# Next batch's preparation on VectorE placed in other blocks of a sparse-attention and expert layer

## The reference

```python
x = x + attention(layernorm(x)); x = x + experts(layernorm(x))

# attention: 8 blocks of 64 tokens; each query block sees itself and its best key block per head
c = einsum(mean of q per block, mean of k per block) * SCALE         # 8 x 8 per head
block_mask = (c >= top-1 of the row) | eye(8)
probs = softmax(where(block_mask, q @ k.T * SCALE, -inf)); out = (probs @ v) @ proj_w.T + proj_b

# experts: 4 experts with 512 hidden features, the 2 best per token
logits = x @ wr + br; gates = softmax(top 2 of logits)
y_e = gelu(x @ w1_e + b1_e) @ w2_e + b2_e
out = sum over the 2 chosen of gate * (y_e - c_e + c_sum)            # c: constants of the biases
```

## Time and profile before

| | |
|---|---|
| median of 3 runs | 943.72 us (943.45 to 947.8) |
| the profiled execution | 946.72 us, of which the span is 945.0 |
| TensorE, matmuls | 876.3 us busy (93% of the span) |
| TensorE, weight loads | 578.6 us (61%) |
| VectorE | 555.0 us (59%) |
| ScalarE | 459.4 us (49%) |
| GpSimd | 181.9 us (19%) |
| mean granted TensorE clock | 0.977 |
| chain that ended last | TensorE 58%, VectorE 15%, issue 10%, DMA 7%, SyncE's queue 5%, ScalarE 3% |

### The profile page before, as it was taken

The page is one execution under the profiler, slowest core; times in us unless marked ns, Lnnn a source line. Parts: engine busy times, 40 slices in busy tenths (PEclk is TensorE's granted clock), DMA queues, the critical chain, the costliest instruction groups (busy, mean ns, idle before and its releaser), DMA issues.

```text
span 945.0 us, 24244 instructions
## 1 busy us (share of the span) xinstructions
PE 876.3 (93%) x9638; PEld 578.6 (61%) x9638; DVE 555.0 (59%) x1554; ACT 459.4 (49%) x740; POOL 181.9 (19%) x183
## 2 busy tenths in 40 slices
PE   3797899999999999999999999999999999999995
PEld 2475666666657666665656666665756666575662
DVE  7445647475675747566574757567474756736321
ACT  1332463645537363644637364463736455373640
POOL 5601110212121121212111121212112121211111
PEclk8797999999999999999999999999999999999998
DMA  7440442615345260625426062533516153350110
GB/s 208 114 135 20 116 132 58 175 34 152 102 117 142 76 167 23 173 80 139 120 78 181 14 190 60 148 110 90 168 40 184 40 148 97 98 149 2 57 57 14
DMA packets 96022, 99.40 MB, mean 105 GB/s; under 512 B 8969, under 2 KB 82705, under 8 KB 95905
## 3 DMA queue, kind: packets, MB, share of 16 engines
q1 hardware_dynamic: 93168, 85.09, 32.5%
q0 software_dynamic: 2544, 12.58, 4.3%
q10 hardware_dynamic: 192, 0.13, 0.1%
HBM read 48.10 MB, written 28.71 MB: 81 GB/s over the span
## 4 chain that ended last, share of the span: by engine, by line
PE 58%; DVE 15%; issue 10%; DMA 7%; SPq 5%; ACT 3%; POOL 1%; DVEq 0%; POOLq 0%; ACTq 0%
PE y_ps L403 14%; PE s_ps L310 8%; PE o_ps L346 5%; SPq L1120 5%; PE s_ps L259 4%; PE s_ps L261 4%; PE s_ps L260 4%; DVE rmax L661 4%; DMA kv<-kv_chosen 3%; ACT hid L949 2%; PE s_ps L335 2%; DMA selected<-kv_table,index 2%; PE v_ps L319 2%; PE v_ps L326 2%; PE a_ps L376 2%
## 5 line engine op out<-in xcount | busy, mean ns | idle before, releaser
L403 PE MATMUL y_ps<-hid,w2s 128*128 128x512 f32 x480 | 240.8, 602 | 0.0
L913 ACT ACTIVATE prob<-s_ps 128x1024 f32<-128x1024 f32 x128 | 131.1, 1024 | 185.4 <-PE s_ps L335 185.4
L661 DVE TRANSPOSE_TENSOR_REDUCE rmax<-s_ps 128x16 bf16<-128x512 f32 x256 | 168.6, 701 | 58.8 <-PE s_ps L310 58.6
L949 ACT ACTIVATE hid<-s_ps,b1s 128x512 f32<-128x512 f32 x256 | 171.1, 688 | 36.5 <-PE s_ps L261 36.0
L310 PE MATMUL s_ps<-qdiag,kv 64*128 64x512 f32 x768 | 134.7, 456 | 7.2 <-DMA kv<-kv_chosen 4.5
L670 DVE TENSOR_REDUCE nmax<-v_ps 128x64 bf16<-128x256 bf16 x128 | 54.0, 422 | 105.4 <-PE v_ps L326 105.4
L259 PE MATMUL s_ps<-xnhi,w1hi 128*128 128x512 f32 x256 | 112.0, 437 | 1.5
L906 ACT COPY vaug<-v_ps 128x128 f32<-128x128 f32 x128 | 34.0, 265 | 162.1 <-PE v_ps L319 156.2
L1049 POOL TENSOR_TENSOR yT<-yT,gate_cols 128x512 f32<-128x512 f32 x48 | 61.6, 1282 | 259.0 <-DVE gate_cols L757 258.6
L310 PEld LDWEIGHTS s_ps<-qdiag,kv 64*128 64x128 f32 x768 | 85.6, 254 | 34.5 <-ACT hid L949 10.6
L261 PE MATMUL s_ps<-xnhi,w1lo 128*128 128x512 f32 x256 | 101.2, 395 | 0.0
(11 more groups left out here) (149 smaller groups left out, 1117.5 us busy)
## 6 DMA issues: line engine op xcount, KB each, us to landing
gate_cols<-gates SPq DMA_DIRECT2D x64, 256.0 KB, 5.2
kv_table<-stage SPq DMA_DIRECT2D x16, 768.0 KB, 3.9
kv<-stage SPq DMA_DIRECT2D x16, 768.0 KB, 6.4
kv_chosen<-selected SPq DMA_DIRECT2D x15, 768.0 KB, 5.3
kv<-kv_chosen SPq DMA_DIRECT2D x15, 768.0 KB, 4.9
qdiag<-qpair SPq DMA_DIRECT2D x504, 16.0 KB
xs<-in_x SPq DMA_DIRECT2D x16, 256.0 KB, 4.4
out_x<-x SPq DMA_DIRECT2D x16, 256.0 KB, 4.8
```

Of the source, the lines that this page charges most:

```text
L403: ins = pe.matmul(dst[:], w2s[:, n, :], hid[:, n, :], start=(c == 0), stop=(c == C - 1))
L661: v.tensor_reduce(rmax[m % 2][:, :, half * P // 2:half * P // 2 + HH].rearrange("p k h -> p h k"), s_ps[m % 2][:, half * N:(half + 1) * N] ...
L913: act.activation(prob[m % 2][:].rearrange("p h s -> p (h s)"), s_ps[m % 2][:], ACT.Exp, scale=SCALE).then_inc(exped, 1)
L949: act.activation(hid[:, k, :], up_ps[up_bank(k)], ACT.Gelu, bias=b1s[:, k:k + 1]).then_inc(gelued, 1)
```

## The change

On VectorE, for b from 1 to 14: a_stats moves from block 0 of the batch before use to the burst one batch earlier (for batch b+2 in the burst of b, between o_project(b, 2) and o_rows(b, 3); for b = 0 behind c_stats). a_rows moves from block 1 (ahead of block_max) to block 0, behind block_max. q's sum and split go from the head of block 3 to block 2 behind block_max and ahead of o_rows; k's from the head of block 4 to block 3 behind block_max; a_select from the head of block 6 to block 5 behind block_max; `qk` goes from block 5 to block 4 and stays ahead of block_max. c_logits goes from block 2 to block 1 behind block_max; a_columns stays in block 1 but ahead of c_gated. c_gates, c_split and c_gates_turned each go one block later. On TensorE the q, k and v projections go from the end of blocks 2, 3 and 4 to behind shift and o_project, a_columns goes between the two c_down of block 1, and a_products goes from the end of block 5 to the end of block 4. GpSimd's inverse and c_split follow. SyncE issues two placements of q fewer ahead of put_selected, two more between it and take_selected, and sends the gates' five transfers after all placements. ScalarE's code is the same.

```diff
--- before.py
+++ after.py
@@ -239,7 +239,7 @@
         def stages(b):
 
 
-            return (2, 0, 1, 3) if b == 0 else (2, 3, 4, 5)
+            return (2, 0, 1, 3) if b == 0 else (2, 3, 4, 4)
 
         def taken(b):
 
@@ -484,8 +484,12 @@
                         o_columns(b, (m - 3) // 2)
                     if m in (4, 6):
                         o_project(b, (m - 4) // 2)
+                    if b >= 1 and b + 1 < B and m in stages(b)[:3]:
+                        project(b + 1, "qkv"[stages(b).index(m)])
                     if b >= 2 and not edge:
                         c_down(b - 2, 2 * m)
+                    if b >= 1 and b + 1 < B and m == 1:
+                        a_columns(b + 1)
                     if m in (2, 4, 6):
                         o_rows(b, (m - 2) // 2)
                     if b >= 2:
@@ -495,9 +499,7 @@
                     if b >= 1 and m == 0:
                         c_route(b - 1, (0, 1))
                     if b + 1 < B:
-                        if b >= 1 and m == 1:
-                            a_columns(b + 1)
-                        if m in stages(b)[:3]:
+                        if b == 0 and m in stages(b)[:3]:
                             project(b + 1, "qkv"[stages(b).index(m)])
                         if m == stages(b)[3]:
                             a_products(b + 1)
@@ -807,14 +809,11 @@
             a_columns(1)
             block_max(0, 0)
             for b in range(B):
+                ahead = b >= 1 and b + 1 < B
                 for m in range(M):
                     row_max(b, m)
-                    if b + 1 < B:
+                    if b == 0:
                         q_at, k_at, _, products_at = stages(b)
-                        if b >= 1 and m == 0:
-                            a_stats(b + 1)
-                        if b >= 1 and m == 1:
-                            a_rows(b + 1)
                         if m == q_at + 1:
                             q_total = a_q_sum(b + 1)
                             a_q_parts(b + 1)
@@ -824,39 +823,53 @@
                             a_qk(max(q_total, k_total))
                         if m == products_at + 1:
                             tied = a_select(b + 1)
-                    if b == 0 and m == 6:
-                        bias_out()
-                    if b == 0 and m == 7:
-                        bias_sum()
-                    if b >= 1:
-                        if m == 1:
-                            c_route(b - 1)
-                        if m == 2:
-                            ranked = c_logits(b - 1)
+                        if m == 6:
+                            bias_out()
+                        if m == 7:
+                            bias_sum()
+                    if b >= 1 and m == 1:
+                        c_route(b - 1)
+                    if ahead and m == 4:
+                        a_qk(max(q_total, k_total))
                     if m + 1 < M:
                         block_max(b, m + 1)
                     if m in (4, 6):
                         o_project(b, (m - 4) // 2)
+                    if ahead and m == 0:
+                        a_rows(b + 1)
+                    if b >= 1 and m == 1:
+                        ranked = c_logits(b - 1)
+                    if ahead and m == 1:
+                        a_columns(b + 1)
+                    if ahead and m == 2:
+                        q_total = a_q_sum(b + 1)
+                        a_q_parts(b + 1)
+                    if ahead and m == 3:
+                        k_total = a_k(b + 1)
                     if m in (2, 4, 6):
                         o_rows(b, (m - 2) // 2)
+                    if ahead and m == 5:
+                        tied = a_select(b + 1)
+                    if b >= 1 and m == 4:
+                        c_gates(b - 1, ranked)
+                    if b >= 1 and m == 6:
+                        c_split(b - 1)
+                    if b >= 1 and m == 7:
+                        c_gates_turned(b - 1)
                     if b >= 2 and m % 2:
                         c_gated(b - 2, m // 2)
                     if b == 0 and m == 2:
                         bias_masked()
-                    if b >= 1 and b + 1 < B and m == 1:
-                        a_columns(b + 1)
-                    if b >= 1 and m == 3:
-                        c_gates(b - 1, ranked)
-                    if b >= 1 and m == 5:
-                        c_split(b - 1)
-                    if b >= 1 and m == 6:
-                        c_gates_turned(b - 1)
                 o_project(b, T - 2)
-                if b == 0 and b + 1 < B:
+                if b == 0:
                     block_max(b + 1, 0)
+                if b >= 1 and b + 2 < B:
+                    a_stats(b + 2)
                 o_rows(b, T - 1)
                 o_project(b, T - 1)
                 c_stats(b)
+                if b == 0:
+                    a_stats(b + 2)
                 c_rows(b)
                 if b >= 2:
                     c_add(b - 2)
@@ -1064,21 +1077,23 @@
             for b in range(B):
                 for m in range(M):
                     if b + 1 < B:
-                        if b >= 1 and m == 0:
-                            inverse(b + 1, mv, veps, rstd, mean_done, rstd_done)
                         if b >= 1 and m == 1:
                             a_rows(b + 1)
                         if m == stages(b)[3] + 1:
                             a_select(b + 1)
                     if b == 0 and m < E:
                         split_w1(m)
-                    if b >= 1 and m == 5:
-                        c_split(b - 1)
                     if b >= 2 and m in (4, 6):
                         c_sum(b - 2, m // 2 - 1)
+                    if b >= 1 and m == 6:
+                        c_split(b - 1)
                 if b >= 2:
                     c_sum(b - 2, E - 1)
+                if b >= 1 and b + 2 < B:
+                    inverse(b + 2, mv, veps, rstd, mean_done, rstd_done)
                 inverse(b, mv2, veps2, rstd2, mean2_done, rstd2_done)
+                if b == 0:
+                    inverse(b + 2, mv, veps, rstd, mean_done, rstd_done)
             b = B - 1
             c_split(b)
             for e in range(1, E):
@@ -1179,23 +1194,20 @@
                         a_v(b + 1, bank_a, bank_a)
                     place_q(b + 1, 0, range(8, H))
                     if b >= 1:
-                        place_q(b + 1, 1, range(4))
+                        place_q(b + 1, 1, range(2))
                     put_selected(b + 1)
-                if b >= 1:
-                    put_gates(b - 1)
                 if b == 0:
                     take_selected(b + 1)
                     place_q(b + 1, 1, range(9))
                 elif b + 1 < B:
-                    place_q(b + 1, 1, range(4, 9))
+                    place_q(b + 1, 1, range(2, 9))
                     take_selected(b + 1)
-                if b >= 1:
-                    for e in range(E - 1):
-                        take_gate(b - 1, e)
                 if b + 1 < B:
                     place_q(b + 1, 1, range(9, H))
                 if b >= 1:
-                    take_gate(b - 1, E - 1)
+                    put_gates(b - 1)
+                    for e in range(E):
+                        take_gate(b - 1, e)
             b = B - 1
             store(b - 2)
             put_gates(b)
```

## The result

The changed kernel takes 949.41 us (median of 10 runs, 947.7 to 951.29) against 943.72 for the kernel before (10 runs). The ratio is 1.0064, 95% interval 1.0052 to 1.0077: slower by about 6 us. Forecast were 950.0 (936 to 961) and slower.

What follows compares the result with a forecast made beforehand. TensorE was taken as the bound, so only stalls could be won: 13 steady batches x 0.83 = 10.8, less 4.5 for the chosen keys, adds 6.3 us; 946.72 profiled becomes 953.0, the runs' median 950.0, range 936 to 961.

Steps and rivals of the forecast that it cites:

- Block 1 and the head of 2: Steady batch: xnlo starts 0.22 late and c_gated(0) adds 0.67 behind it, so nmax(2) is 0.89 us late.
- att before weighted(2): Block 2: att comes only after q's sum and split, so weighted(2) waits and its delay reaches 1.35 us.
- relief wins: Rival: block 2's delay of 1.35 us vanishes, batches gain 0.52 and the kernel is faster, 932 us; chance 0.14.
- Products behind the v copy: Block 4: TensorE's a_products wait for ScalarE's v copy, queued behind values(b, 5); cost 1.23 us per batch.
- VectorE's k split and o_project: Blocks 4 and 6: stalls of 1.00 us each, from k's split and selection ahead of block_max and o_project, are won.
- Selection at 1.80: Block 5: the keys' selection takes 1.80 us instead of 2.44, as L627 no longer runs beside GpSimd's L1035.
- `qk` product: Block 4: it meets GpSimd's sum of gated(1); block_max(5) begins at worst 0.6 us late, hidden before values(5).
- The chosen keys: TensorE's 4.5 us of waits on the chosen keys' DMA go, bounds 0 to 4.5.
- TensorE's lateness of 0.83 us: Steady batch: weighted(6) comes 0.83 us late, which was to cover the chosen keys' transfer.
- The ends: The first two batches and the last, outside the 13 steady ones, are left at 0 +/- 2 us.
- no new wait: Rival: the change wins 2.00 us in each of 13 batches and the keys' 4.5 us, 913 us; chance 0.02.

Runs made afterwards that it cites:

- e3: The changed kernel with c_gated(0) back ahead of xnlo in VectorE's block 1; ratio 0.9991 to the kernel before.
- e2: The changed kernel with VectorE's o_rows of block 2 placed between q's sum and q's split; ratio 1.0003 to the kernel before.
- e1: The changed kernel with ScalarE copying v to stage before the values in block 4 of batches 1 to 14; ratio 0.9880 to the kernel before.
- e7: The kernel of e5 with VectorE's c_gated(2) moved from block 5 to behind row_max(6); 912.64 us, ratio 0.9650 to the kernel before.
- e4: The kernel before with only c_split moved from block 5 to block 6 on VectorE and GpSimd; ratio 0.9902 to the kernel before.
- e5: The changed kernel with the three orders of e1, e2 and e3 turned at once; 915.59 us, ratio 0.9696 to the kernel before.

## Why the prediction was right

*Block 1 and the head of 2, +0.89.* Measured 0.83: weighted(1) to shift(2) went from 1.80 to 2.63. vaug and xnhi start at 526.30 and 526.47, where the forecast, shifted by 1.90, has 526.31 and 526.52; e3 shows that the gating's place is 0.65 of the price.

*att before weighted(2), +0.46* (1.35 less 0.89). Measured 0.48 to 0.50 by what e2 removes. The rival "relief wins" needed this and the step before to be hidden: neither was.

*Products behind the v copy, +1.23.* From values(5) to weighted(4) it takes 544.55 - 542.82 = 1.73 in the changed kernel and 528.69 - 528.32 = 0.37 in e1: 1.36, and e1's distances are 1.35 shorter; 14 batches have it, 18.9 us, which agrees with the 17 of the runs inside their intervals. The vaug and the v copy were priced right: the copy ends 1.31 behind values(5), where 1.33 was forecast. Of the 0.13 more, 0.09 lies between the end of the copy and weighted(4), which took 0.42 where 0.33 was put, and 0.06 in the order without the wait, which takes 0.37 where 0.43 was put; the copy gave 0.02 back. It was the largest new wait, and it rested on the order of three queues.

*VectorE's k split and o_project, -1.00 in block 4 and -1.00 in block 6.* Both came. The waits on `x` went from 15.2 us to 0.2. In block 6, 0.24 came back through nmax(6), where 0.28 was worked out; e7 removed it. In block 4 the relief was larger than priced: with the products' wait gone, in e1, weighted(3) to (4) takes 528.69 - 523.12 = 5.57 with the products in it, where 5.75 was forecast. This 0.18 is why that stretch came out at +0.34 in the changed kernel though the wait alone was 0.13 above its price: two small errors cancelled.

The prediction puts the whole 1.00 of block 4 down to the k split, and that isn't shown. The gates stood ahead of nmax(4), from 534.63 to 536.02, and half of this was the collision above. By these instants, which makes it an estimate, nmax(4) could have started about 0.7 sooner without them, since row_max(4) ends on TensorE at 535.26, and the listed waits of that block, 0.26 at shift(4) and 0.50 at values(5), would have been nearly gone with the k split left in its place. No run moves one without the other.

*Selection at 1.80.* Measured 549.43 - 547.65 = 1.78, L627's successor L629 at 0.226 us in the median. The Trainium skill (SBUF — State Buffer, section "Who interferes with whom") says that a VectorE instruction with two SBUF inputs contends with a GpSimd instruction that reads SBUF. The traces agree in each place where such a pair was moved apart or together: L627, in the changed kernel and in e4; the gates' product, 0.86 us beside GpSimd's sum and 0.19 without it; and the `qk` product, which now meets GpSimd's sum of gated(1). There `qk` holds block_max(5) up by about 1.0 us, where the prediction had 0.6 at worst, and values(5) still doesn't wait:

```profile
538.96 1.20 DVE L619 TENSOR_TENSOR qk<-qsum,ksum 128x64 f32<-128x64 f32 x1
540.08 1.31 DVE L663 TRANSPOSE_TENSOR_REDUCE rmax<-s_ps 128x16 bf16<-128x512 f32 x2
541.31 0.25 DVE L691 TENSOR_TENSOR x<-v_ps,xs 128x128 f32<-128x128 f32 x1
```

*The chosen keys, -4.5.* Measured -3.8 of listed waits. The size was right and the reason half right. I let TensorE's lateness of 0.83 us cover the transfer. But in e5 TensorE isn't late and still doesn't wait: the take goes out 6.82 us ahead of scores (548.30 - 541.48), where it was 5.4 and 4.9 us at the ends of two neighbouring bursts in the kernel before. What does it is the selection one block earlier. The index and the scores that need its keys, before and then in the changed kernel:

```profile
548.81 0.21 DVE L636 TENSOR_SCALAR index<-cbest,rbase 128x1 uint32<-128x1 f32 x1
```

```profile
566.62 1.03 PE L310 MATMUL s_ps<-qdiag,kv 64*128 64x512 f32 x6
```

```profile
549.30 0.22 DVE L638 TENSOR_SCALAR index<-cbest,rbase 128x1 uint32<-128x1 f32 x1
```

```profile
569.21 1.03 PE L310 MATMUL s_ps<-qdiag,kv 64*128 64x512 f32 x6
```

From the end of one to the start of the other it is 17.60 us before, 19.69 in the changed kernel and 19.71 in e5. So the lateness of 0.83 gives nothing: the delays of blocks 1 to 4 hold up the index and the scores alike. The two added placements take only part of the 2.1 back: the take goes out 12.1 to 12.7 us behind the index in most batches before, and 12.5 to 13.5 in e5.

*The ends, 0 +/- 2.* The last batch gained 0.98 us: before, its shift(4) waited 0.70 us for nmax(4) behind the gates, whose product was held there too, and after the change this wait is gone. By the sum of steady batches (13 x 0.47 = 6.1) less this, 5.1 us are explained of the 6.0 that the ratio gives (4.9 to 7.3 by its interval); the remaining 0.9 is within the interval, and what the first two batches add was not tried by itself. So part of the closeness of 950.0 is luck: without the keys the steady batches cost 13 x 0.75 = 9.8, which is 1.0 less than the 10.8 forecast, and the keys' waits gave 0.7 less than the 4.5 they were priced at.

So the step most worth learning is the sum. Per batch about 2.2 us of stall were removed, plus the keys' wait, and 2.9 were added in four places (0.83, 0.48, 1.36 and 0.24), the largest of them in a queue that the edit left alone. The rival "no new wait" was priced at 913, 0.967 of the kernel before; with the order turned in all four places, e7 came to 0.965.

## What to carry to other kernels

When an instruction of one engine is moved ahead, ask for each buffer that it waits for who frees it and what stands before that in *that* engine's queue; here four new waits cost more than VectorE's relief brought. ScalarE's unchanged order was nearly half of them, and turning two calls gave that back. Work put behind the urgent instruction of one block can still stand ahead of the next urgent one: its length has to be compared with the idle time before that, block by block. Look at an instruction whose median is about four times its shortest before moving what is around it: in this kernel the excess belonged to another engine, both at L627 and at the gates' product, and moved with it.

## What was not expected of the hardware

The `qk` product in GpSimd's way took 1.20 us, against 0.216 in the median before, and it began 0.16 us after the start of GpSimd's sum of 1.28 us (538.80) and ended 0.08 us behind it. A cast with a single input, which the sentence on two inputs doesn't cover, was held as well: in e4 L706 took 1.20 us in the 13 batches where it overlapped GpSimd's sum and 0.42 in the three where it did not. In all these places the waiting shows in the profile as a longer instruction, and not as idle time.
